# Where blocks 1 and 2 of an additive attention end in a feed-forward stream

## The reference, cut to what matters

```python
h    = tanh(txt_proj[:, None] + feat_proj[:, :, None] + b)   # rows x 77 tokens x 512
rho  = einsum('bftd,d->bft', h, w) + masked                  # a score per row and token
att  = softmax(rho)
txt_h = einsum('bft,btd->bfd', att, ctx)
w_s, b_s = tanh(txt_h @ Wcw + bcw), tanh(txt_h @ Wcb + bcb)  # two numbers per row
x = x + w_s * layernorm(x) + b_s
y = silu(fp4(ln(x)) @ fp4(w_gate).T) * (fp4(ln(x)) @ fp4(w_up).T)
x = x + fp4(y) @ fp4(w_down).T                               # inner size 1408
```

## Time and profile before

| what | value |
|---|---|
| median of 3 runs | 1595.73 us (1595.61 to 1597.28) |
| profiled execution, its own time | 1594.65 us |
| profiled execution, span of its instructions | 1592.8 us |
| PE busy | 1448.8 us, 91% |
| ACT busy | 1356.7 us, 85% |
| DVE busy | 1218.2 us, 76% |
| POOL busy | 245.4 us, 15% |
| mean granted TensorE clock | 0.98 |

### The profile page before, as it was taken

How to read it: one execution, slowest core, us unless ns; L and a number is a source line. 1 busy time by engine, 2 the same in 40 slices (tenths; PEclk the granted TensorE clock), 3 DMA queues, 4 the chain that set the end, 5 groups by cost and what they waited for, 6 DMA issues and landing times.

```text
span 1592.8 us, 24368 instructions
## 1 busy us (share of the span) xinstructions
PE 1448.8 (91%) x9752; PEld 641.4 (40%) x9752; DVE 1218.2 (76%) x1991; ACT 1356.7 (85%) x1223; POOL 245.4 (15%) x406
## 2 busy tenths in 40 slices
PE   6988888865999899999999999999999999799997
PEld 3334444411333333343443433434434343455554
DVE  6589998765586566779787677797876777899885
ACT  5999999999999999999999999999999998123331
POOL 1122222110111011011111111011101111121220
PEclk9989999989999999999999999999999999899999
DMA  4133333330011111202111111112211111132332
GB/s 140 40 81 86 80 80 78 75 75 12 8 26 39 39 26 39 39 14 39 39 39 39 39 39 39 39 32 46 39 39 36 36 35 36 38 68 61 76 70 56
DMA packets 180789, 77.91 MB, mean 49 GB/s; under 512 B 163883, under 2 KB 163883, under 8 KB 180677
## 3 DMA queue, kind: packets, MB, share of 16 engines
q1 hardware_dynamic: 179984, 75.00, 21.1%
q10 hardware_dynamic: 693, 1.36, 0.3%
HBM read 27.85 MB, written 8.39 MB: 23 GB/s over the span
## 4 chain that ended last, share of the span: by engine, by line
PE 64%; ACT 23%; DVE 10%; DMA 1%; issue 1%; POOL 0%; SPq 0%; ACTq 0%; DVEq 0%; POOLq 0%
PE rho L719 24%; ACT hring L561 17%; PE dn L808 10%; PE gu0g L796 5%; PE gu1g L796 5%; PE gu1u L796 5%; PE gu0u L796 5%; ACT hring L556 5%; PE gu1u L746 1%; PE gu1g L746 1%; PE gu0u L746 1%; PE gu0g L746 1%; DVE work L914 1%; DVE featT L883 1%; DVE sm L902 1%
## 5 line engine op out<-in xcount | busy, mean ns | idle before, releaser
L561 ACT ACTIVATE hring<-featT,bias 128x1024 f32<-128x1024 f32 x936 | 985.8, 1137 | 28.1 <-PE rho L719 28.1
L719 PE MATMUL rho<-hring,wslide 128*32 128x512 f32 x4928 | 599.1, 611 | 103.9 <-ACT hring L561 94.0
L719 PEld LDWEIGHTS rho<-hring,wslide 128*32 128x32 f32 x4928 | 134.2, 110 | 452.9 <-issue 241.9
L556 ACT ACTIVATE hring<-featT 128x4096 f32<-128x4096 f32 x72 | 259.8, 3609 | 7.3 <-DVE featT L883 5.1
L808 PE MATMUL dn<-wd_room,turned 128*128 128x512 f16 x1023 | 233.3, 380 | 0.0
L463 POOL TENSOR_SCALAR split_t<-sm 128x88 f32<-128x88 f32 (+2 forms) x91 | 22.2, 244 | 1192.3 <-DVE sm L905 1192.3
L883 DVE TENSOR_SCALAR featT<-featT,bias 128x1024 f32<-128x1024 f32 x288 | 197.4, 750 | 5.3 <-ACT hring L561 2.2
L1173 DVE TENSOR_TENSOR work<-sg,gu1u 128x352 f32<-128x352 f32 x64 | 33.4, 521 | 163.8 <-ACT sg L581 163.4
L808 PEld LDWEIGHTS dn<-wd_room,turned 128*128 128x128 f16 x1023 | 95.0, 98 | 155.6 <-issue 51.1
L796 PE MATMUL gu0g<-wg,turned 128*128 128x352 f16 x768 | 128.1, 317 | 14.2 <-DVE work L1173 14.2
L796 PE MATMUL gu0u<-wu,turned 128*128 128x352 f16 x768 | 125.7, 314 | 0.0
(11 more groups left out here) (171 smaller groups left out, 1361.2 us busy)
## 6 DMA issues: line engine op xcount, KB each, us to landing
xt<-in_x SPq DMA_DIRECT2D x32, 256.0 KB, 2.8
out<-xt SPq DMA_DIRECT2D x32, 256.0 KB, 2.5
work<-in_x SPq DMA_DIRECT2D x10, 512.0 KB, 3.9
xt<-in_x SPq DMA_DIRECT2D x6, 512.0 KB, 3.7
xt<-in_L_ffn_w_gate SPq DMA_DIRECT2D x11, 256.0 KB, 2.7
xt<-in_L_ffn_w_up SPq DMA_DIRECT2D x11, 256.0 KB, 2.7
work<-in_L_ffn_w_down SPq DMA_DIRECT2D x2, 704.0 KB, 4.3
xt<-in_L_ffn_w_down SPq DMA_DIRECT2D x2, 704.0 KB, 4.3
```

What stands on the lines that cost most here:

```text
L556: act.activation(hring[:, s // 2, :, 0:rows], featT[:, :, r:r + rows], ACT.Tanh).then_inc(tanh_ready, GRP)
L561: act.activation(hring[:, s // 2, g, (s % 2) * 512:(s % 2) * 512 + rows], featT[:, e, ROW0[k]:ROW0[k] + rows], ACT.Tanh, bias=bias[:, e, b ...
L719: last = pe.matmul(rho[SLOTW * g:SLOTW * g + SLOTW, hf * 512:hf * 512 + 512], wslide[:, e, SLOTW - 1 - r:2 * SLOTW - 1 - r], hring[:, s // ...
```

## The change

Blocks 1 and 2 no longer end behind gate_up(t, 2) of tile `BASE[k] - 2`, but behind piece 6, the last third of the down product, of the same tile. Their softmax runs within the next tile (`LATE_AT`: tiles 7 and 15). Block 3 still ends at (22, 2) as before, but begins at (15, 0) instead of (14, 3). So block 1 is spread over 46 pieces instead of 42, block 2 over 56 as before, block 3 over 52 instead of 56. Quads per tile, counted from the planner's rule:

```diff
-        t0, p0 = (0, 0) if k == 1 else (BASE[k - 1] - 2, 3)
-        t1 = BASE[k] - 2
+        t0, p0 = (0, 0) if k == 1 else (BASE[k - 1] - 1, 0)
+        t1, p1 = BASE[k] - 2, 2 if k == NBLK - 1 else 6
         mine = [(t, p) for t in range(t0, t1 + 1) for p in range(7)
-                if (t, p) >= (t0, p0) and (t, p) <= (t1, 2) and not (t == 0 and p >= 4)]
+                if (t, p) >= (t0, p0) and (t, p) <= (t1, p1) and not (t == 0 and p >= 4)]
...
-    SOFTMAX_AT = {BASE[k] - 2: k for k in range(1, NBLK)}
+    SOFTMAX_AT = {BASE[NBLK - 1] - 2: NBLK - 1}
+    LATE_AT = {BASE[k] - 1: k for k in range(1, NBLK - 1)}
...
                     if t - 1 in SOFTMAX_AT and n == 0:
                         softmax_gates(SOFTMAX_AT[t - 1])
+                    if t in LATE_AT and n == 2:
+                        softmax_gates(LATE_AT[t])
                     silu_gate(t, n)
+                    if t in LATE_AT and n == 0:
+                        tanh_quad(issued)
+                        issued += 1
+                        softmax_exp(LATE_AT[t])
...
                         softmax_transposes(SOFTMAX_AT[t], 0)
-                    for n in slots.get((t, p), ()):
+                    if t in LATE_AT and p == 0:
+                        softmax_transposes(LATE_AT[t], 0)
+                    for i, n in enumerate(slots.get((t, p), ())):
                         score_quad(n)
+                        if t in LATE_AT and p == 0 and i == 0:
+                            softmax_transposes(LATE_AT[t], 1)
...
                 ending = SOFTMAX_AT.get(t - 1)
+                if t in LATE_AT:
+                    softmax_drain(LATE_AT[t])
+                    hidden(t, 0)
+                    softmax_shift(LATE_AT[t], 0)
+                    softmax_shift(LATE_AT[t], 1)
+                    softmax_sums(LATE_AT[t])
+                    hidden(t, 1)
+                    softmax_factors(LATE_AT[t])
+                    hidden(t, 2)
+                    rows_tile(t + 1)
+                    hidden(t, 3)
+                    quantise_hidden(t)
+                    result(t - 1)
+                    restart()
+                    continue
```

## The result

The changed kernel is slower: 1602.35 us median of 5 runs (1601.02 to 1603.66) against 1595.68 us (1594.62 to 1597.28), ratio 1.0040 with a 95% interval of 1.0027 to 1.0054. That is 6.7 us, beyond the 3.2 us that can be told from nothing. It lies inside the range given, but its size is that of rival 1 (slower, 1601 us, chance 0.26) and not that of the forecast, which was no difference.

A forecast was written before the change was run, and what follows sets the result against it. ACT's idle time up to the last tanh was taken to bound the kernel. Seams +4.5, clock +0.4, sum wait -3.5, block 3 -3, block 1 +1, block 2 +0.5 gave -0.1: forecast 1595.8 us, range 1589.5 to 1603.

The forecast's parts named there:

- rival 1: Slower, 1601 us: the new stall at the seams is larger than walked, seams +8 and clock +2.15; chance 0.26.
- the start of tile 23: Sign expected in the profile after: tile 23 starts where it did, to within 3 us.
- What bounds the kernel: Up to the last tanh quad, near 1350 us, every microsecond that ACT idles is a microsecond of the kernel.
- The walk of the seam: At each new seam PE idles 5.2 us before the second transposes; ACT idles 4.0 against 1.75 before, net +4.5 us.
- PE's late start: At the second seam the drain ends near T + 4.8; PE loses 1 us, which the next wait swallows.
- three thin margins: Behind the seam, operands for the next gate_up, sum 165 and the next gate bank all fit, with 0 to 1.4 us spare.
- The clock: One fall of PE's clock in two seams, costing 1.7 less the 1.25 of before: +0.4 us, bounds -1.25 and +5.5.
- The case with both falls: PE's clock falls at both seams: 3.4 less the 1.25 of before, +2.15 us.
- The step that failed: Block 1 takes 11 us more PE work into a room of 25; its 1.1 us of score waits grows by about 1.
- The sum's wait: In block 1, ACT's 3.52 us wait at 533 us for a sum from DVE goes: -3.5 us, bounds -4.1 and 0.
- blocks 2 and 3: ACT's waits for scores: block 2 +0.5 us; block 3 falls from 5.6 to about 2.8, -3 us.
- Rival 2: Faster, 1589 us: full relief of block 3 and the sum wait, seams only +3, no clock fall; chance 0.20.

The follow-up runs named there:

- e8: Changed kernel with the sum taken out of hidden(t, 0) in the late tiles and made between DVE's two shifts: 1591.75 us, ratio 0.9976 to the kernel before.
- e2: Changed kernel with DVE's shift of half 0 moved ahead of hidden(t, 0) and its sum in the late tiles: 1590.32 us, ratio 0.9962 to the kernel before.
- e1: Changed kernel with one quad moved from piece (2, 6) back to (1, 0): 1598.33 us, ratio 1.0018 to the kernel before.
- e4: Kernel before the change with one quad moved from piece (1, 0) to (1, 4): 1600.75 us, ratio 1.0029 to the kernel before.
- e5: Changed kernel with only block 1 ending late, block 2 then having 52 pieces: 1597.36 us, ratio 1.0012 to the kernel before.
- e6: Changed kernel with only block 2 ending late, block 2 then having 60 pieces: 1597.51 us, ratio 1.0013 to the kernel before.
- e7: Kernel before the change with one quad moved from (2, 5) to (2, 4), so quad 116 is summed one call earlier: 1590.78 us, ratio 0.9965.
- e3: Changed kernel with one quad moved from (2, 6) to (1, 0) and the shift ahead of hidden(t, 0): 1587.45 us, ratio 0.9945 to the kernel before.

## Why the prediction was right or wrong

**The number.** The forecast was no difference, and the measured time is 6.7 us longer by the medians. By the places in the table of idle times the change is +9.8 against a sum of -0.1: 6.0 are tile 1, which no term had, 2.0 the seams, 1.6 the rest of block 1. That the time still fell into the range is in part luck, since no bound in it covered tile 1. The last silu of tile 22 came 7.5 us later, where I had said at most 3 for the start of tile 23.

**What bounds the kernel** held: ACT's idle time before the last tanh is the kernel's time. Every experiment that took ACT waits away shortened it. Nothing shows that a wait was given back later: the part behind tile 22 took 237.5 to 240.8 us in the ten kernels, 237.5 in the changed kernel as in e8.

**The walk of the seam** was right in its structure and to 0.1 us up to the second transposes, and e2 and e8 show that its cause, hidden(t, 0) and the sum ahead of the shift, is the right one. One small thing was missed: at the second seam PE's late start was not swallowed by the next wait, it cost ACT 0.78 us through the ring. The three thin margins behind it (gates, `xqT`, sum 165) held: none of them shows as a wait.

**The clock** is the term that was mis-sized. I took one fall of 1.7 us in two seams, +0.4. It fell at both, and at the first it cost 0.8 us on the transposes and 2.1 on the gate piece, 2.9; at the second 0.8 and 0.5. Less the 1.25 of before that is +2.95, if all of it reaches ACT; ACT's waits without it are 3.8 and 3.6 us, where the walk had 4.0 for each. The case with both falls was priced at +2.15, the sentence on the Trainium skill pointed to it, and the row at 728 us, a fall after waits of about 2 us, should have weighed more than the second seam's lack of one. The two seams together cost +6.9 instead of +4.9. A third fall, in tile 1, was in no term.

**The step that failed** is "Block 1 gets these 11 us, into a room of 25: its 1.1 grows by about 1, at most 3". I reasoned from the mean room of PE in the whole block. But a planner that spreads 70 quads over 46 pieces instead of 42 also takes a quad out of (1, 0), the first piece of the first full tile, and there PE meets DVE, which is still busy with quantise_hidden(0). The before trace had the hint: PE waited 1.2 us for hidden(1, 0) at 446 us, with two quads in (1, 0). I did not ask what happens when PE comes a quad's time sooner: the wait is 5.0 us and the clock falls behind it. It was worth 3.5 to 4.5 us by e1 and e4, over half of the 6.7. The rest of block 1 grew by 2.6 where I had about 1, inside my upper bound of 3.

**The sum's wait** (-3.5) and **blocks 2 and 3** (+0.5 and -3 against +0.3 and -2.5) were right, and e5, e6 and e7 confirm their mechanisms.

**Rival 1** came true in size, though only half by its mechanism: its place was the seams, and it had +8 and +2.15 for the clock there, 10.15, against +6.9; the rest came from tile 1. It priced the seams too high and did not have tile 1, so its total fits by luck. **Rival 2**, a faster kernel, is what e3 is (1587.45 against its 1589), but with no stall at the first seam at all and a relief of block 3 of about 2.5 to 3 us, not 5.6.

**Slips in the working.** A direct quad is (680.50 - 672.18) / 2 = 4.16 us; the silu lies ahead of that stretch and nothing is to be taken off. The 11.1 us that leave block 3 are one gate piece and the three down pieces of tile 14. Neither moves the forecast.

## What to carry to other kernels

When work is moved between two transposes, products or shifts that share one buffer, look at what the in-order engine between them does in that slot. A 2.7 us addition whose result was first read 20 us later (705.0 to 725.2 us in the changed kernel) held PE, and with it everything queued behind, and the clock that fell behind this wait of PE added to its cost.

When a proportional planner gets other bounds, every slot moves, the ones at the far end too. Look at each place where the trace of before already has a small wait, and ask what a quad less or more before it does; mean room in the stretch did not show it here.

## What the runs showed of the hardware

The lower clock came after shorter waits than I had assumed. In e8 PE waited 2.48 us and the next gate half took 3.3 us to the start of the next (702.76 to 706.10) instead of 1.8. Over the ten traces, from 405 to 1345 us, all eleven waits of PE of 4.1 to 5.1 us, in tile 1 and at the seams, were followed by slower matmuls. Of twelve waits of 2.23 or 2.24 us, seven were. The kernel before has such a wait at both seams, each behind one of 1.23 us, and the clock fell at the first; e7 has the same two waits and it fell at the second. One row with a fall (e2) and one without (e7):

```profile
1045.22 3.57 PE L726 MATMUL rho<-hring,wslide 128*32 128x512 f32 x16 [2.23 <-ACT hring L562]
...
722.22 1.92 PE L726 MATMUL rho<-hring,wslide 128*32 128x512 f32 x16 [2.23 <-ACT hring L568]
```

So the same wait in the same place cost nothing in one execution and 1.6 to 1.7 us of PE's time in another, and one of 5.0 us in tile 1 cost between 1.4 and 2.7 us on the gate piece. It fits with this that the runs of one kernel lie up to 8 us apart and follow their mean granted clock. What decides in the single case, no run here shows. The Trainium skill ("TensorE: Matmul & The Clock Gate", section on HAM oscillation) warns of idle gaps between bursts; the eleven long waits agree, while the shorter ones brought the lower clock only in part of the cases. The cost in the clock's part was up to 2.9 us for one wait of 5.1.
